# Weights' sums of squares by TensorE, the output product from float16 pairs, and new orders in an attention and FFN kernel

## The reference, cut to what matters

```python
def _layernorm(x, eps=1e-05):
    return (x - mean(x)) / sqrt(var(x) + eps)
def attn(hidden, wq, wkv, wo):      # S=1024, HID=512, H=32 heads, DN=DV=128, DQ=192
    q = (hidden @ wq).reshape(B, S, H, DQ)
    kv = hidden @ wkv               # k: first H*DN columns, v: the next H*DV
    scores = einsum('bqhd,bkhd->bhqk', q[..., :DN], k) * DQ ** -0.5
    probs = softmax(where(causal, scores, -1e30))
    return einsum('bhqk,bkhd->bqhd', probs, v).reshape(B, S, H * DV) @ wo
def ffn(x, k0, s0, k1, s1, k2, s2): # kernels are 512x512 of +1/-1
    h = relu(s0 * (x @ w0)) * 2
    h = relu(s1 * (exc_inh(h) @ w1)) * 2
    return s2 * (exc_inh(h) @ w2)   # exc_inh: the last 20% of rows times -4
x = x + attn(_layernorm(x), wq, wkv, wo)
x = x + ffn(_layernorm(x), k0, s0, k1, s1, k2, s2)   # x is [1, 1024, 512], all float32
```

## Time and profile before

| | |
|---|---|
| runs | 1138.97, 1137.42, 1138.96 us; median 1138.96 us |
| profiled execution | 1138.74 us, of which the span is 1136.9 us |
| busy of the span | PE 1092.0 us (96%), PEld 655.2 (58%), DVE 895.9 (79%), ACT 678.0 (60%), POOL 667.6 (59%) |
| granted TensorE clock | 0.998 over the span |
| DMA | 118.25 MB, queue share 52.5% of the 16 engines |

### The profile page before, as it was taken

How to read it: one execution, slowest core, us unless ns; L and a number is a source line. 1 busy time by engine, 2 the same in 40 slices (tenths; PEclk the granted TensorE clock), 3 DMA queues, 4 the chain that set the end, 5 groups by cost and what they waited for, 6 DMA issues and landing times.

```text
span 1136.9 us, 18752 instructions
## 1 busy us (share of the span) xinstructions
PE 1092.0 (96%) x6223; PEld 655.2 (58%) x6223; DVE 895.9 (79%) x1797; ACT 678.0 (60%) x1334; POOL 667.6 (59%) x682
## 2 busy tenths in 40 slices
...
GB/s 157 88 99 84 119 108 128 100 116 94 96 112 109 121 114 114 82 117 109 91 121 114 124 82 119 112 76 121 117 130 89 117 107 81 118 93 115 92 1 75
DMA packets 367584, 118.25 MB, mean 104 GB/s; under 512 B 313088, under 2 KB 361344, under 8 KB 367488
## 3 DMA queue, kind: packets, MB, share of 16 engines
q1 hardware_dynamic: 367488, 117.05, 52.5%
...
...
## 4 chain that ended last, share of the span: by engine, by line
PE 75%; DVE 12%; issue 6%; ACT 4%; POOL 3%; DMA 0%; SPq 0%; POOLq 0%; ACTq 0%; DVEq 0%
PE psC L1108 42%; PE psS L1108 16%; PE psC L1231 16%; DVE p L975 3%; DVE qk L907 2%; POOL wqk L487 2%; ACT raw L674 2%; POOL wqk L484 1%; DVE res L991 1%; DVE attn L958 1%; ACT attn L728 1%; DVE bound L930 1%; DVE psS L968 0%; DVE bound L936 0%; DVE bound L933 0%
## 5 line engine op out<-in xcount | busy, mean ns | idle before, releaser
L1108 PE MATMUL psC<-xb,wqk 128*128 128x512 f16 x1356 | 328.1, 381 | 12.5 <-POOL wqk L487 10.9
L706 ACT ACTIVATE psS<-psS,negmax 128x128 f32<-128x128 f32 (+7 forms) x256 | 182.8, 714 | 221.3 <-DVE negmax L968 220.4
L1108 PE MATMUL psC<-wos,attn 128*128 128x512 f32 x768 | 253.5, 441 | 13.5 <-DVE attn L958 10.1
L968 DVE CUSTOM_DVE_ANT_0 psS<-psS,mask,undo_qk 128x128 f32<-128x128 f32 (+7 forms) x256 | 208.4, 820 | 62.2 <-PE psS L1108 60.5
L975 DVE SCALAR_TENSOR_TENSOR p<-psS,p 128x128 f16<-128x128 f32 (+7 forms) x256 | 192.6, 752 | 60.2 <-ACT p L714 57.1
L1108 PE MATMUL psS<-qkT 128*128 128x512 f16 (+3 forms) x1152 | 230.0, 327 | 1.2 <-DVE p L975 0.7
L1108 PEld LDWEIGHTS psC<-xb,wqk 128*128 128x128 f16 x1356 | 124.5, 98 | 160.3 <-issue 36.3
L1231 PE MATMUL psC<-pT,v 128*128 128x512 f16 (+3 forms) x1152 | 197.8, 326 | 0.0
L991 DVE SCALAR_TENSOR_TENSOR res<-psC,rinv,res 128x512 f32<-128x512 f32 x256 | 190.1, 743 | 9.3 <-DVE rinv L982 8.1
L1108 PE MATMUL psC<-wvs,xb 128*128 128x256 f16 x1536 | 188.5, 273 | 0.4 <-POOL wvs L487 0.4
L484 POOL TENSOR_TENSOR wqk<-raw,one 128x512 f16<-128x512 f32 x122 | 115.9, 950 | 110.4 <-ACT raw L674 97.8
...
## 6 DMA issues: line engine op xcount, KB each, us to landing
...
pT<-p SPq DMA_TRANSPOSE x256, 4.3
...
```

What stands on the lines that cost most here:

```text
L706: nc.scalar.activation(row, row, ACT.Exp, bias=negmax[:, n:n + 1], scale=-1.0, accum_out=rowsum[:, j % 2, n:n + 1]) \
L968: nc.vector.tensor_tensor_reduce(row, row, mask[:, S - width:S], undo_qk[:, j % 2:j % 2 + 1], 3e38, ALU.add, ALU.min, negmax[:, n:n + 1]). ...
L1108: last = nc.tensor.matmul(out_ap, w, x, start=k == 0, stop=k == len(terms) - 1)
```

## The change

- `put`, `get`, the DRAM buffer and the reduction L930 go. In their place PE multiplies a 128x128 float32 block of ones (a broadcast) by the column `wmax` (`add_rows`, step `add`; `spread` at the start alike): each is one float32 matmul of 1 or 2 columns that leaves the total on every partition. DVE's `sc` reads it from PSUM.
- The output product is made from float16 pairs. `wo` is loaded for both heads of a pair at once, and gets its own sum of squares (`mx2`), bound (with that of the values) and scaling (`r2`) on ACT. The attention result goes from PSUM to float32 SBUF on ACT (`pv`, `keep_pv`), from there to the high part on ACT (`ah`) and to the low part on POOL (`al`). DVE's `pv` goes. What undoes the scales is multiplied into the inverse row sums (`rv`, L979 ff.).
- The first head's q and k products are done in halves of 256 columns (`ya`, `yb`), each as soon as two row tiles are there.
- 34 float32 matmuls of the identity by itself run at PE's start, 10 ahead of the first `spread`, 24 behind it.
- All orders and the steady banks are new. At the end pv1, `ah`, o4 to o7 of the last head come last.

```diff
 TENSOR_ORDERS = ("""
-    pv1@-1 s4@0 v0@0 s5@0 v1@0 x3@1 v2@0 s6@0 v3@0 x4@1 s7@0 x5@1 o4@-1 x6@1 o5@-1 x7@1 v4@0 o6@-1 x1@2 v5@0 s0@1
-    x2@2 o7@-1 s1@1 pv0@0 s2@1 v6@0 o0@0 s3@1 o1@0 v7@0 o2@0 s4@1 o3@0 s5@1 pv1@0 s6@1 x3@2 s7@1 o4@0 x4@2 o5@0 x5@2
-    x6@2 o6@0 x7@2 o7@0 pv0@1 x1@3 o0@1 s0@2 o1@1 s1@2 x2@3 o2@1 s2@2 o3@1 s3@2""", """
...
+    pv1@-1 s3@0 add1@0 x3@1 s4@0 x4@1 s5@0 x5@1 o4@-1 x6@1 s6@0 v0@0 add0@2 s7@0 v1@0 x7@1 o5@-1 v2@0 o6@-1 v3@0
+    x1@2 o7@-1 s0@1 x2@2 s1@1 pv0@0 v4@0 s2@1 v5@0 s3@1 v6@0 o0@0 s4@1 o1@0 v7@0 o2@0 s5@1 pv1@0 o3@0 s6@1 x3@2 o4@0
+    x4@2 o5@0 s7@1 o6@0 add0@3 o7@0 x5@2 pv0@1 x6@2 x7@2 x1@3 o0@1 o1@1 s0@2 x2@3 o2@1 s1@2 o3@1 s2@2""", """
+    spread1@2 ya0@2 yb0@2 v0@2 spread2@2 ya1@2 turn4@2 v1@2 turn5@2 yb1@2 turn6@2 turn7@2 ya2@2 v2@2 s0@2 s1@2 yb2@2
+    s2@2 ya3@2 yb3@2 s3@2 y4@2 v3@2 s4@2 v4@2 s5@2 y5@2 s6@2 v5@2 s7@2 y6@2 add0@4 y7@2 v6@2 add1@2 v7@2""", "")
 SCALAR_ORDERS = ("""
...
+    e6@-1 h6@-1 mx1@0 e7@-1 r0@1 h7@-1 pv0@-1 ah0@-1 qk3@0 qk2@0 snap0@1 e0@0 h0@0 qk1@0 e1@0 e2@0 mx2@0 h1@0 h2@0
+    pv1@-1 ah1@-1 e3@0 h3@0 r1@0 e4@0 h4@0 qk0@1 e5@0 h5@0 mx0@2 e6@0 v0@0 h6@0 v1@0 qk1@1 r0@2 qk3@1 e7@0 qk2@1
+    v2@0 h7@0 v3@0 r2@0 e0@1 snap0@2 h0@1 e1@1 pv0@0 ah0@0 v4@0 h1@1 e2@1 v5@0 h2@1 e3@1 h3@1 v6@0 mx0@3 qk0@2 v7@0
+    e4@1 e5@1 h4@1 h5@1 pv1@0 ah1@0""", """
+    nhi0@2 mx1@2 keep0@2 nhi1@2 nhi2@2 r1@2 nhi3@2 vhi0@2 vhi1@2 keep1@2 mx0@3 root1@2 v0@2 y0@2 keep2@2 nhi4@2
+    keep3@2 r0@3 nhi5@2 y1@2 keep4@2 nhi6@2 keep5@2 nhi7@2 v1@2 keep6@2 keep7@2 e0@2 h0@2 v2@2 e1@2 h1@2 y2@2 e2@2
+    part0@2 h2@2 y3@2 e3@2 h3@2 y4@2 part1@2 v3@2 v4@2 e4@2 h4@2 e5@2 h5@2 part2@2 mx2@2 y5@2 e6@2 mx0@4 v5@2 h6@2
+    e7@2 y6@2 r0@4 h7@2 part3@2 v6@2 y7@2 v7@2 r2@2""", "")
 VECTOR_ORDERS = ("""
...
+    o0@-1 m0@0 o1@-1 l0@0 o2@-1 m1@0 m2@0 a2@1 l1@0 l2@0 m3@0 o3@-1 sc1@0 l3@0 m4@0 a3@1 m5@0 a4@1 l4@0 a5@1 rv0@0
+    l5@0 m6@0 o4@-1 a6@1 m7@0 v0@0 sc0@2 v1@0 l6@0 a7@1 o5@-1 o6@-1 v2@0 l7@0 m0@1 v3@0 m1@1 o7@-1 a2@2 l0@1 m2@1
+    l1@1 m3@1 v4@0 l2@1 v5@0 o0@0 l3@1 v6@0 m4@1 v7@0 m5@1 o1@0 l4@1 l5@1 o2@0 o3@0 m6@1 a3@2 o4@0 a4@2 o5@0 m7@1
+    o6@0 sc0@3 l6@1 a5@2 l7@1 a6@2 a7@2 o7@0""", """
+    nlo0@2 sc1@2 nlo1@2 nlo2@2 stat4@2 stat5@2 stat6@2 stat7@2 scale1@2 nlo3@2 rest1@2 apply4@2 sc0@3 apply5@2 y0@2
+    apply6@2 nlo4@2 apply7@2 nlo5@2 y1@2 nlo6@2 nlo7@2 v0@2 v1@2 m0@2 sum0@2 l0@2 m1@2 v2@2 m2@2 l1@2 sum1@2 y2@2
+    m3@2 l2@2 y3@2 sum2@2 l3@2 part0@2 m4@2 y4@2 m5@2 v3@2 l4@2 part1@2 l5@2 m6@2 part2@2 y5@2 v4@2 m7@2 v5@2 sc0@4
+    l6@2 sum3@2 y6@2 l7@2 v6@2 part3@2 v7@2 sc2@2 y7@2""", "")
 SYNC_ORDERS = ("""
...
+    lv0@0 t0@-1 t1@-1 t2@-1 t3@-1 t4@-1 t5@-1 lqk0@2 t6@-1 lo0@0 t7@-1 t0@0 t1@0 t2@0 t3@0 t4@0 t5@0 lqk0@3 t6@0
+    t7@0""", """
+    t0@2 t1@2 lo0@2 t2@2 t3@2 lqk0@4 t4@2""", "")
 POOL_ORDERS = ("""
-    sum0@1 qk0@1 wv2@0 wqk0@2 qk2@1 qk1@1 qk3@1 wo0@0 sum0@2 wv0@2 wv1@2 qk0@2 wqk0@3 wo0@1 qk2@2 qk1@2 qk3@2""", """
+    qk0@0 wo0@-1 wqk0@1 al0@-1 qk3@0 qk2@0 sum0@1 qk1@0 al1@-1 wv0@0 wv1@0 qk0@1 qk1@1 wqk0@2 qk2@1 wv2@0 wo0@0
+    al0@0 qk3@1 sum0@2 al1@0""", """
     wqk0@2 wk0@2 wv0@2 wv1@2 wqk0@3 wk0@3""", "")
...
-BANKS = "301230123012301201230120123012301230123012"
+WARM = (10, 24)
+
+BANKS = "012301230123012301230123012301201230120120123"
...
             def split_out(g, j):
-                wait(pool, loaded["o"], g, 16, j, 16)
+                wait_pair(pool, scaled[2], g, 1, j, 1)
                 wait(pool, done["o"], g, 8, j, 0)
-                nc.gpsimd.tensor_tensor(wos[:, HI, :], raw[:, 4, :], one[:, :].to_broadcast([P, D]), ALU.mult) \
-                    .then_inc(wo_hi, 1)
-                wait(pool, wo_hi, g, 1, j, 1)
-                nc.gpsimd.tensor_tensor(wos[:, LO, :], raw[:, 4, :], wos[:, HI, :].bitcast(F32), ALU.subtract) \
-                    .then_inc(wo_lo, 1)
+                split(raw[:, 6 + j % 2, :], wos[:, HI, :], wos[:, LO, :], wo_hi, wo_lo, lambda: wait(pool, wo_hi, g, 1, j, 1))
+
+            def attention_lo(g, j, c):
+                wait(pool, hi_done["pv"], g, 2, j, c + 1)
+                nc.gpsimd.tensor_tensor(attn[:, LO, :], attn32[:, c, :], attn[:, HI, :], ALU.subtract)                     .then_inc(lo_done["pv"], 1)
...
-            def pv_hi(g, j, c, bank):
+            def keep_pv(g, j, c, bank):
                 wait(act, done["pv"], g, 2, j, c + 1)
+                wait(act, lo_done["pv"], g, 2, j, c - 1)
+                nc.scalar.activation(attn32[:, c, :], psC[:, bank, :], ACT.Copy, scale=PV_DOWN).then_inc(pv_kept, 1)
+
+            def attention_hi(g, j, c):
+                wait(act, pv_kept, g, 2, j, c + 1)
                 wait(act, done["o"], g, 8, j, 4 * c)
-                if j % GH == 0 and c == 0:
-                    wait_pair(act, undo_ready, g, 1, j, 1)
-                nc.scalar.activation(attn[:, HI, :], psC[:, bank, :], ACT.Copy, scale=undo_v[:, :]) \
+                nc.scalar.activation(attn[:, HI, :], attn32[:, c, :], ACT.Copy) \
                     .then_inc(hi_done["pv"], 1)
...
                 w = wait_pair if n else wait
-                total, root, inverse, scale = (bound[:, at, k:k + 1] for k in range(4))
-                if isinstance(g, int) and (GH * g + j <= 1 or n and g + j // GH == 0):
+                root, inverse, scale = (bound[:, k, a:b] for k in range(1, 4))
+                if isinstance(g, int) and (n == 0 and GH * g + j <= 1 or n == 1 and first):
                     k = (0, 2)[GH * g + j] if n == 0 else 1
                     dve.wait_ge(spread_done, k + 1)
-                    rows = psC[:, 3, k * P:(k + 1) * P]
+                    total = psC[:, 3, k:k + 1]
                 else:
-                    w(dve, rows_in[n], g, 16, j, 0 if n else -16)
-                    rows = wrow[:, at, :]
+                    w(dve, rows_added[min(n, 1)], g, 1, j, 1 if n else -1)
+                    total = psC[:, bank_at(g, "add", j, min(n, 1)), 0:1]
+                    if n:
+                        total = psC[:, bank_at(g, "add", j, 1), n - 1:2]
...
-                wait_pair(dve, bounded[1], g, 4, j, 4)
-                wait_pair(dve, lo_done["pv"], g, 2 * GH, j, 0)
-                nc.vector.tensor_scalar_mul(undo_v[:, :], bound[:, 2, 1:2], 2.0 ** (67 - W_UP) / UP).then_inc(undo_ready, 1)
+                wait_pair(dve, bounded[1], g, 3, j, 3)
+                if isinstance(g, int) and g + j // GH == 0:
+                    dve.wait_ge(bounded[2], 3)
+                wait(dve, rinv_done, g, 1, j, 0)
+                nc.vector.scalar_tensor_tensor(undo_o[:, :], bound[:, 1, 2:3], 2.0 ** (141 - 2 * W_UP), bound[:, 1, 3:4],
+                                               ALU.mult, ALU.mult).then_inc(undo_ready, 1)
...
+                nc.vector.reciprocal(rowinv[:, :], rowsum[:, j % 2, :]).then_inc(inverse_done, 1)
+                wait(dve, inverse_done, g, 1, j, 1)
+                wait_pair(dve, undo_ready, g, 1, j, 1)
+                nc.vector.tensor_scalar_mul(rinv[:, :], rowinv[:, :], undo_o[:, :]).then_inc(rinv_done, 1)
...
-                nc.tensor.transpose(psC[:, 3, k * P:(k + 1) * P], wmax[:, at:at + 1].to_broadcast([P, P]),
-                                    ident[:, :]).then_inc(spread_done, 1)
+                nc.tensor.matmul(psC[:, 3, k:k + 1], one[:, 0:1].to_broadcast([P, P]), wmax[:, at:at + 1],
+                                 start=True, stop=True).then_inc(spread_done, 1)
+
+            def add_rows(g, j, n, bank):
+
+                if n:
+                    wait_pair(pe, rows_max[1], g, 1, j, 1)
+                    wait_pair(pe, rows_max[2], g, 1, j, 1)
+                    at, count = 2, 2
+                else:
+                    wait(pe, rows_max[0], g, 1, j, 1)
+                    at, count = j % 2, 1
+                nc.tensor.matmul(psC[:, bank, 0:count], one[:, 0:1].to_broadcast([P, P]),
+                                 wmax[:, at:at + count], start=True, stop=True).then_inc(rows_added[min(n, 1)], 1)
...
+            def plain_half(step, t, bank):
+
+                n, cols = TILED[step, t - t % 2], slice(t % 2 * 2 * P, (t % 2 + 1) * 2 * P)
+                a = (A11, S2)[n % 2]
+                if t % 2 == 0:
+                    pe.wait_ge(plain_lo if n % 2 else first_lo, 1)
+                pe.wait_ge(xt_lo, 2 * t + 2)
+                terms = []
+                for d in range(DC):
+                    terms += halves(lambda w: wqk[:, w, a + d // 2, d % 2, :],
+                                    lambda w: xb[:, 2 * (n // 2) + d // 2, w, d % 2, cols])
+                last = chain(psC[:, bank, cols], terms)
+                if t % 2:
+                    last.then_inc(plain_done, 1)
...
             pe.wait_ge(const_ready, 1)
+            for t in range(WARM[0]):
+                nc.tensor.matmul(psT[:, t % 4, 0:P], ident[:, :], ident[:, :], start=True, stop=True)
             spread(0)
+            for t in range(WARM[1]):
+                nc.tensor.matmul(psT[:, t % 4, 0:P], ident[:, :], ident[:, :], start=True, stop=True)
```

189 lines of the change are left out of this document (88 added, 101 removed).

## The result

The changed kernel takes 1106.11 us (median of 4 runs, 1105.43 to 1106.94) against 1138.89 (4 runs, 1137.42 to 1138.97): ratio of the runs 0.9715, 95% interval 0.9699 to 0.9732. Forecast was 1109.5, with an own range of 1101 to 1117 and 1096 to 1127 with the rivals; 32.8 us came, where 29.4 were forecast. The profiled execution took 1104.8 us from first to last instruction; before it was 1136.9.

What follows compares the result with a forecast made beforehand. PE bounds the kernel; a steady pair falls from 65.65 to 62.3 + 0.5 + 0.6 + 0.3 = 63.7 us. Fourteen pairs -27.3, start -1.5, first pair -2, end +1.4 give 1109.5 us (1101 to 1117; with rivals 1096 to 1127).

Steps and rivals of the forecast that it cites:

- fifth rival: Output chains keep their extra cost in float16 too: 65.3 us a pair, 1134 us in all; chance 3%.
- The POOL sequence: POOL's work from wo to `sum0` takes 17.0 us against PE's 16.6, so x3 waits: 0.5 us a pair (0.2 to 1.0).
- The adds: Three float32 add matmuls a pair on PE, taken at 0.2 us each: 0.6 us a pair (0.3 to 1.35).
- Other waits: PE waiting at add0@2 for mx0@2, at other adds and for banks DVE reads last: 0.3 us a pair (0 to 1.5).
- PE waits for none of them now, so nothing: Steady pair: transposes may come earlier without put and get on the SP queue, but PE never waits for them: 0 us.
- Start and first pair: Outside the fourteen pairs: start -1.5 us (-4 to +6), first pair and other pairs outside -2 us (0 to -3).
- I give the warming nothing for y0: At the start: PE idles before ya0, the clock falls again, so the warming matmuls gain no time there.
- End: Last head: o0's operand path is 1.0 us longer, and 0.4 more after the last pv1: +1.4 us (0 to +4).
- the first (waits come back): Cheaper chains, but PE meets similar waits at new places: 64.6 us a pair, 1122 us in all; chance 20%.
- The second: Adds are dear at 0.45 us each, warming matmuls slow too: 64.5 us a pair, 1125 us in all; chance 8%.
- The third: Nearly all of PE's waits go: 62.7 us a pair, 1095 us in all; chance 17%.
- slower one: POOL's sequence bounds because al0 starts late, deciding from 2 us; at 3 us 66.7 a pair, 1151 us; chance 7%.

## Why the prediction was right

*The period.* It was put at 62.3 + 0.5 + 0.6 + 0.3 = 63.7, and is 63.56. Part of that closeness is luck: the terms were off by +0.1, -0.2 and -0.2 us. They came out as follows.

- Columns and the o chains at them, 62.3: measured 62.36, and the extra of the float32r chains is gone. The fifth rival is refuted.
- *The POOL sequence*, 0.5: measured 0.64, as 0.34 at x3 and 0.30 at s0. Size and reason were nearly right. The prediction placed all of it on POOL's own row from o7; with x7 first, which takes the other path away, 0.58 is left, and the doubled al0 costs 0.97, so that row explains nearly all of it. What the prediction did not see is the second path, from x7 over a7, ACT and qk2, that ends at the same time: in the trace, and in the run with al0 on DVE, which made it 0.9 longer.
- *The adds*, 0.6: measured 0.42. I took 0.2 each, and it is 0.14. By the rule of the Trainium skill that I weighed (FP8 and Floating Point Precision, section TensorE Precision Notes: four passes for true float32) the prediction estimated up to 0.45 for an add. The price isn't borne out: an add shows as two pairs of weight load and matmul, and takes 0.14 with both. The rule itself isn't contradicted: the warming matmuls of 128 columns start 0.22 apart, four times the 0.055 of a float16 matmul of 128 columns (s0, three from 919.52). What failed in the estimate is its base, the 0.11 of a transposing matmul of 128 columns, since an add has one or two.
- *Other waits*, 0.3: none in a quiet pair, since 62.36 + 0.64 + 0.42 is 63.42 of its 63.43. In their place 0.13 in the mean of late transposes, against the sentence "PE waits for none of them now, so nothing". That was argued from the kernel before, whose pair was 2 us longer; this step failed. It was worth 2 us of the total, shown by the loads behind t7.

*Which part did it.* The prediction gave the float16 chains 1.6 us a pair. In the old order they bring 1.0, because waits, that for the q and k weight among them, take the place of part of what they free. The new orders, the adds and the banks together bring the other 1.1 a pair. These were not tried apart, so which of them gives how much stays open; the trace shows only that the adds cost 0.4 of it back.

*Start and first pair.* Forecast -3.5, measured -4.9. The ten warming matmuls start 0.43 apart and are through when the first spread comes, at 6.95 (6.8 was worked out), 1.1 later than before, as forecast. The squares that the spread waits for on ACT:

```profile
5.72 0.19 ACT L694 ACTIVATION_READ_ACCUMULATOR squares<-raw 128x1 f32 x1
```

They are there at 5.91, and before and without warming the spread came 0.14 behind them; so 0.9 of the 1.1 is the warming, and the other 0.2 an input that landed later. In the run without warming the spread came at 6.66, since there the squares themselves waited for their input and ended at 6.52. These landings differ by up to 1.3 us between the profiles (squares from 4.53 to 5.82), so the spread's time in that run doesn't price the warming.

One reading of the rows was wrong: y0's 12 matmuls from 17.98 to 22.19 are 0.35 each in the mean, not 0.43. The trace has them 0.38 to 0.43 apart for the first eight and 0.22 for the last four, so the 0.43 is right for the slow ones only.

"I give the warming nothing for y0" was wrong on the pace: ya0 and yb0 took 2.78 us here, and 4.56 without warming. It was close on the time, since v0 then waited 1.34 for its weights. The run with the loads behind t7 has the same start, and there the two took 4.43 and v0 started at 21.87, only 0.16 later; so the warming doesn't hold the pace every time, and little hangs on it. The granted clock (the column behind POOL's, as in the earlier trace rows) of the run with the loads behind t7, and then of y0 in the kernel before:

```profile
18.00:22.00 4.00, 4.00 (x24) 2.90 (x22) 3.96 (x11) 3.55 (x8) 2.27 (x2) 0.57 0.01 4
```

```profile
17.98:22.30 4.32, 4.32 (x13) 1.66 (x14) 2.68 (x9) 2.86 (x8) 0.00 (x0) 1.00 0.00 0
```

In the first the column fell with the pace, near the lower of its two levels (1.2 of 2.4 GHz). In the second it reads 1.00 while most of the matmuls go at half pace, as it does for the ten slow warming matmuls. So in the first microseconds of a profile the starts of the rows are the safer reading.

The rule of the Trainium skill (TensorE: Matmul & The Clock Gate, part 1), that idle time lets the clock fall again, is borne out by the whole products: 5.53 us of idle, then 12 matmuls of 256 columns in 2.74 us at a granted clock of 0.50, where they take 1.47 in the stream. A shorter idle stretch doesn't settle it. Ahead of ya0 PE was idle 1.41 us both in the changed kernel and with the loads behind t7, and only the second lost its pace. Ahead of the last head's o0 it was idle 3.34 and 3.35 us; the 12 matmuls behind it took 2.75 in the first and 4.33 in the second. The prediction took such a fall as given from the kernel before, where 2.31 us of idle was followed by 4.4.

*End.* Forecast +1.4, measured +1.9. o0 of the last head waits 3.34 for al0, "over 3 us" as written; before it was 2.31. The chain behind it kept its full pace in this profile, which wasn't foreseen and isn't so in every run, as said above.

*Engines.* DVE 50.4 a pair (49 forecast), ACT 43.5 (44.3), POOL 46.8 (47.2).

Of the rivals, the first (waits come back) is true of the float16 pairs without the new orders. The second needed adds of 0.45, and they take 0.14. The third (62.7 a pair) wasn't reached by any variant; the best quiet pair is 63.15. The slower one needed al0 2 us late, and al0 started without a wait (POOL, 915.90).
